# Four-layer convolution kernel on one core: the copies of the planes' edges behind layer 0's first loads, and the box's first part behind the transforms' products

## What is computed

```python
def reference(x, ...):
    x = x + _L0_conv_ref(_gn(x), ...)   # 1x1 and 3x3 convolution, product of 8x8 FFTs, normalization over channels
    x = x + _L1_conv_ref(_gn(x), ...)   # 1x1, FFT with a mask, 3x3, gelu gate
    x = x + _L2_conv_ref(_gn(x), ...)   # integral image, four gathered corners a pixel: the "box"
    x = x + _L3_conv_ref(_gn(x), ...)
    return x

def _gn(v, G=16, eps=1e-5):
    m = jnp.mean(g, axis=(2, 3, 4), keepdims=True)   # over the whole image
    s = jnp.var(g, axis=(2, 3, 4), keepdims=True)
    return ((g - m) / jnp.sqrt(s + eps)).reshape(v.shape)
```

## Time and profile before

| | before |
|---|---|
| median of three runs | 20823.17 us |
| lowest, highest | 20798.16, 20833.35 us |
| profiled execution | 20805.98 us |
| its span | 20804.4 us |
| PE, DVE, ACT, POOL busy | 91%, 64%, 36%, 50% |
| PE's granted clock, mean | 0.962 |

### The profile page before, as it was taken

How to read it: one execution, slowest core, us unless ns; L and a number is a source line. 1 busy time by engine, 2 the same in 40 slices (tenths; PEclk the granted TensorE clock), 3 DMA queues, 4 the chain that set the end, 5 groups by cost and what they waited for, 6 DMA issues and landing times. The chain is left out here.

```text
span 20804.4 us, 500656 instructions
## 1 busy us (share of the span) xinstructions
PE 18912.8 (91%) x172464; PEld 11734.2 (56%) x172464; DVE 13400.9 (64%) x22319; ACT 7497.1 (36%) x22720; POOL 10324.5 (50%) x8692
## 2 busy tenths in 40 slices
PE   6998998989999989899999898999997889898999
PEld 4665555466655554566555546665555456565666
DVE  4444445666667776666677766666777677777744
ACT  4664332155542221555422215553322122222222
POOL 0000000077767740777677407776773088787800
PEclk9999999999999999999999999999999999999999
DMA  3331112655544446555344465553444666666633
GB/s 94 72 72 44 36 37 92 135 114 116 114 102 113 114 126 137 116 120 119 100 113 112 129 134 118 119 120 101 113 116 128 136 145 147 151 150 148 151 87 77
DMA packets 932864, 2323.52 MB, mean 112 GB/s; under 512 B 276340, under 2 KB 528504, under 8 KB 844124
## 3 DMA queue, kind: packets, MB, share of 16 engines
q1 hardware_dynamic: 500560, 1364.68, 28.1%
q0 software_dynamic: 430080, 928.96, 16.9%
HBM read 1915.53 MB, written 385.13 MB: 111 GB/s over the span
## 5 line engine op out<-in xcount | busy, mean ns | idle before, releaser
L1842 POOL DMA_INDIRECT e_got<-table,e_idx x6144 | 7483.8, 1218 | 2376.3 <-issue 1624.3
L1858 POOL DMA_INDIRECT e_got<-table,e_idx x2048 | 2539.9, 1240 | 690.1 <-issue 537.0
L1012 PE MATMUL b_p_conv<-b_z,b_diag 32*32 32x512 f32 x76032 | 2810.7, 599 | 0.0
L531 PE MATMUL a_p_qk<-a_wst,a_stack 125*128 125x192 f32 x12288 | 2463.9, 337 | 273.0 <-ACT a_qh L662 212.3
L531 PEld LDWEIGHTS a_p_qk<-a_wst,a_stack 125*128 125x128 f32 x12288 | 2023.2, 191 | 709.0 <-issue 438.6
L1114 ACT ACTIVATE b_z<-b_p_z 128x256 f32<-128x256 f32 x2112 | 845.0, 400 | 3875.9 <-PE b_p_z L976 3522.7
L1896 DVE TENSOR_TENSOR e_got<-e_got,e_wt 128x1536 f32<-128x1536 f32 x1024 | 1779.0, 1753 | 698.5 <-DMA e_got<-table,e_idx 646.3
L976 PEld LDWEIGHTS b_p_z<-const,b_ym 128*128 128x128 f32 x8448 | 1149.8, 196 | 1199.0 <-issue 696.9
L1201 DVE TENSOR_TENSOR b_ym<-b_p_in,b_mask 128x512 f32<-128x512 f32 x1056 | 729.9, 691 | 1653.1 <-PE b_p_in L968 1652.9
L976 PE MATMUL b_p_z<-const,b_ym 128*128 128x128 f32 x8448 | 1524.7, 304 | 100.2 <-ACT b_z L1114 94.0
L2142 PE MATMUL d_p_v<-d_xs,d_ws 125*128 125x512 f32 x4608 | 1379.7, 447 | 59.7 <-issue 56.2
(11 more groups left out here) (291 smaller groups left out, 35717.4 us busy)
## 6 DMA issues: line engine op xcount, KB each, us to landing
e_got<-table,e_idx POOLq DMA_INDIRECT x8192
b_x<-planes SPq DMA_DIRECT2D x264, 395.1 KB
a_stack<-in_xp SPq DMA_DIRECT2D x256, 387.0 KB
c_stack<-planes SPq DMA_DIRECT2D x256, 387.0 KB
d_stack<-planes SPq DMA_DIRECT2D x512, 193.5 KB
table<-i_acc SPq DMA_DIRECT2D x256, 384.0 KB, 2.3
b_xr<-planes SPq DMA_DIRECT2D x264, 197.5 KB
planes<-b_out SPq DMA_DIRECT2D x264, 197.5 KB
```

What stands on the lines that cost most here:

```text
L531: m = pe.matmul(dst_, st[:, row, dx + 128 * t:dx + 128 * t + 128], wst[:, dx, 0:2 * C2], start=(dx == 0), stop=False)
L1012: mm = pe.matmul(p_conv[q // 2 * 2 + r % 2][BLK * c:BLK * (c + 1), :], diag[g][BLK * r:BLK * (r + 1), k, :], zs[BLK * r:BLK * (r + 1), g, ...
L1842: pool.indirect_dma_start(out=self.got[q][:, t, c * REC:(c + 1) * REC], out_offset=None, in_=self.flat, in_offset=bass.IndirectOffsetOnAxi ...
L1858: pool.indirect_dma_start(out=self.got[q][:, t, c * REC:(c + 1) * REC], out_offset=None, in_=self.flat, in_offset=bass.IndirectOffsetOnAxi ...
```

## The change

The six copies are taken out of the first block, with SP's wait for them. They become a function `set_edges`, which `layer0` of image 0 calls on SP right behind the first loads of `others`. The wait for the six stands at the end of SP's stream in that call. On DVE the box's part is called from two places: in steps with a back it stands where it stood, and in the first step, which has none, behind the two products.

```diff
-def layer0(env, src, dst, p, b, boxes=None, stats=None):
+def layer0(env, src, dst, p, b, boxes=None, stats=None, edges=None):
...
                         sp.dma_start(t[:], planes(src, i + 1, 0, CP, 1, SROWS)).then_inc(others_loaded[i], 16)
+                if edges:
+                    edges[0](sp)
...
                 for k in range(2):
                     sp.wait_ge(stored[k], ((b + 1) * U + 1) * 16)
+                if edges:
+                    sp.wait_ge(edges[1], 96)
...
+                def box_parts(u, k):
+                    for part in ((1, 2) if k % 2 else (0,)):
+                        boxes.part(dve, u, k // 4, k // 2 % 2, part)
+
                 def step(u, k, n, front, back, back2, turn_box):
...
-                    if boxes and front:
-                        for part in ((1, 2) if k % 2 else (0,)):
-                            boxes.part(dve, u, k // 4, k // 2 % 2, part)
+                    if boxes and front and back:
+                        box_parts(u, k)
...
                             dve.tensor_tensor(prod[k % 2][:, h, :, :].rearrange("p t c -> p (t c)"), bank[0:NPROD, 0:4 * C2],
                                               qh[:, h, :, :].rearrange("p t c -> p (t c)"), ALU.mult).then_inc(prod_ready, 1)
+                        if boxes and not back:
+                            box_parts(u, k)
...
                 sp.dma_start(const[:], cst).then_inc(const_loaded, 16)
-
-                for t in (p1, p2):
-                    sp.dma_start(t[:, :, 0, :], xp[:, :, 0, :]).then_inc(edges, 16)
-                    sp.dma_start(t[:, :, H + 1:H + 10, :], xp[:, :, H + 1:H + 10, :]).then_inc(edges, 16)
-                    sp.dma_start(t[:, 0, 1:H + 1, :], xp[:, 0, 1:H + 1, :]).then_inc(edges, 16)
                 sp.wait_ge(const_loaded, 16)
-                sp.wait_ge(edges, 96)
...
+        def set_edges(sp):
+
+            for t in (p1, p2):
+                sp.dma_start(t[:, :, 0, :], xp[:, :, 0, :]).then_inc(edges, 16)
+                sp.dma_start(t[:, :, H + 1:H + 10, :], xp[:, :, H + 1:H + 10, :]).then_inc(edges, 16)
+                sp.dma_start(t[:, 0, 1:H + 1, :], xp[:, 0, 1:H + 1, :]).then_inc(edges, 16)
...
-            layer0(env, xp, p1, args("a_"), 0, stats=stats)
+            layer0(env, xp, p1, args("a_"), 0, stats=stats, edges=(set_edges, edges))
```

## The result

The changed kernel takes **20777.66 us** (median of 14 runs, 20764.94 to 20791.91), the kernel before, run beside it, 20819.13 (14 runs). The ratio is 0.9979, with a 95% interval of 0.9971 to 0.9987: 41.5 us, or 0.21%, faster. A second series of the same two gave 0.9983 (0.9974 to 0.9992), 34.1 us. Forecast were 33.5 us less and a median of 20786, in a range of 20760 to 20814.

The account below looks back on a forecast made before the run. The start was taken to be bound by SP's wait for six copies, the first three steps of `layer0` with boxes by the gathers. 32.0 + 0 + 1.5 = 33.5 us less, median 20786, range 20760 to 20814.

Parts of the forecast that it names:

- The start: First block: without the wait for the six copies, the first load comes at 6.4 to 6.8 us, 32.0 us earlier.
- The copies' new place: Behind the first `others` loads in image 0's `layer0`: copies cost zero, margin 2.6 us, up to 10 us as upper end.
- Rival (a): In `layer0` of image 0, the copies make the next `others[0]` late beyond DVE's slack, costing up to 10 us; chance 13%.
- Rival (c): Copies share DMA engines with loads issued before them; the first step's `others[0]` lands at 219, 37.5 us lost; chance 4%.
- Part two: `weigh` behind the products in the first step of three `layer0` calls with boxes: 1.5 us gained in all.
- small term: First steps of `layer0` with boxes: 32nd gather 0.5 to 0.7 us earlier; 0.5 a call taken, 1.5 us in all.
- The 7.4 us of the second step: PE turns the second step's result at about 4228.0 instead of 4235.37; worth nothing, as the third step waits for gathers.
- Rival (b): In the three `layer0` calls with boxes the 7.4 us come through, gaining 3 x 6.5 us more; chance 8%.
- within 2: Sign: time from the first step's second `weigh` to the third step's, 25.35 us, should stay within 2 us of that.
- bound of 2 us a call: Bounds given for the reordered `weigh` in each `layer0` call with boxes: -2 and +2 us.
- The clock: PE starts third and fourth steps colder after idling; each could cost 1.5 to 3 us, covered by gather wait and slack.
- rival (d): In the three `layer0` calls with boxes the cold clock outweighs the gather's half microsecond, +2 us a call; chance 7%.

## Why the prediction was right, and where it was not

**The start: right.** The first load at 6.50 us lies in the forecast 6.4 to 6.8, with no wait for the copies. At the statistics' end only 26.1 of the 32 us were there, since the stage took 107.5 us from the first load on, against 101.5 before. The traces give no sign that the change causes that: with the two other runs of the old start it took 107.2 and 105.1, and with the other starts like the change's between 98.0 and 105.6. It scatters by itself, on waits of one or two microseconds for loads.

**The copies' new place: right, with a little more room than forecast.** They cost DVE's first step nothing (16.11 us against 15.24, 16.42 with the copies elsewhere). The last copy ended at 191.5 and the next `others[0]` landed at 193.9. With the 25.6 us added by which DVE's first read had moved, that is 217.1 and 219.5 in the old time, where 219 and about 222 were forecast. The margin was 4.9 us instead of 2.6. Rival (a) was a real mechanism: at the call's end it cost 9.71 us, and with twice the copies 27.57. There the load behind the copies waited for the four engines. By the Trainium skill (DMA: Bandwidth & Descriptors, "Why a DMA increments its semaphore by 16 and not by 1") a DMA takes the lowest-numbered engines, so that the four are among the seven. These traces agree: three of the load's seven engines were done some 19 us ahead of the other four, and with the copies late it was 39.9 us from the first copy to the load's landing against 39.3 worked out. Rival (c) fell for loads already issued: these earlier loads weren't held up. The same copies ahead of them cost 29.5 us.

**Part two: the mechanism right, the small term mis-sized.** The 7.4 us of the second step came through there: the turning begins 10.37 us behind the 16th gather (4207.13 - 4196.76), before 17.80, so 7.43 us earlier. The third step again waited for the 32nd gather, and nothing of the 7.4 was left by itself. Rival (b), 6.5 us a call, doesn't come: the third step's turning is 2.85 us earlier against the 16th gather (30.55 against 33.40). The step that failed is the one that said "I take 0.5 a call". I had spread 5.3 us of overrun evenly over 10 us of DVE work, and moved only the 1.3 us of `lower` out of the stretch. The overrun lies in single issues instead, and what counts is which operations follow each other. The first long issue went from 3.51 to 1.49 us and the one of the third step from 2.86 to 1.45, while one new overrun of 0.43 came. That makes 2.02 + 1.41 - 0.43 = 3.0, less 0.1 on the others: 2.9 us in the first call; by the intervals between the two `weigh` the three calls have 3.0, 2.5 and 2.9, together 8.4. Each is outside the "within 2" that I had given, and outside the bound of 2 us a call. Added to 32.0 it makes 40.4, near the 41.5 of the first series; the second, 34.1, doesn't confirm it, and no time here settles whether the 8.4 reach the end. Nor do the traces: counted from the 16th gather, the seventh step's turning is 2.5, 1.6 and 2.8 us earlier with the change, but 2.8, 0.8 and 0.4 with the box's part alone.

**The clock.** It behaved as feared, and most of its price was covered. Behind both waits PE was granted 0.50, which is 1.2 GHz. The two stretches of the changed kernel, from the turning in the second step and in the third:

```profile
4207.00:4211.00 4.00, 3.87 (x14) 3.78 (x15) 1.71 (x3) 1.59 (x4) 2.92 (x4) 0.50 0.26 74
4227.00:4231.00 4.00, 3.69 (x13) 3.60 (x14) 3.40 (x6) 1.77 (x4) 3.08 (x4) 0.50 0.26 74
```

Before, the same work behind the second step's turning was granted 1.00, in this stretch:

```profile
4235.00:4239.00 4.00, 3.63 (x24) 3.05 (x24) 3.56 (x5) 1.83 (x5) 3.39 (x3) 1.00 0.27 74
```

and 0.63 behind the third's. For the work from the second step's turning up to its next wait PE took 14.6 us (4207.13 to 4221.73), before 12.8; these 1.8 us lie ahead of the wait of 5.58 us and cost nothing. In the fourth step nothing covers them: from the third step's turning to the fourth's 14.25, 14.43 and 14.90 us went by in the three calls, before 13.58, 13.38 and 13.65. These 0.7 to 1.3 us are a part of rival (d)'s price, and less than what the gathers gave. Other runs of the same order took 13.3 to 14.8 us there, so it isn't paid every time.

**The numbers.** 20786 for 20777.66; 35% had been given to faster by over 0.2%, 63% to within 0.2%. The result, 0.21%, sits on that border. The 7 us by which part two was too small are about the distance between forecast and result. But that the forecast's median lies so near to both series, 8.3 us over the one and 3.3 under the other, is in part luck: medians of the same kernel are 12 us apart.

## What to carry to other kernels

A DMA that nothing needs soon goes behind the loads that are needed now, at a place where the queue is otherwise empty; ahead of one of them it cost here nearly all that its removal from the start had won. Reckon the copies' end against the next load behind them, since the margin is lost there first, in time on the shared DMA engines. Where an engine's wait is removed and a stream of transfers binds behind it, ask when that stream begins: the order of `weigh` was worth about 3 us a call, and the load that starts the gathers, moved to the head of its queue, about 20.

## What the runs showed of the hardware

**Held-up issues of gathers.** In the stretch of gathers 16 to 32 an indirect DMA's issue on POOL takes 0.95 us, but 1.27 to 3.51 where it begins beside DVE's operations with two inputs in SBUF, or just ahead of one, and each of the long ones ends 0.83 us behind the end of a DVE operation. Over the whole trace of the kernel before, 2668 of 8192 issues are longer than 1.04 us, the longest 6.91, and 2604 of these end 0.82 to 0.84 us behind such an end. For example, with the change 4200.52 + 1.49 = 4202.01, and the `weigh` ended at 4199.43 + 1.76 = 4201.19; with the weighing in the middle 4209.89 + 2.89 = 4212.78, and the `weigh` ended at 4210.21 + 1.75 = 4211.96. Mostly it is the operation that ran as the issue began (2284 of the 2668). The longest issues of the stretch passed it by: the last one began beside `a_t` (until 4210.29) and ended with the `weigh` behind it, and the old one of 3.51 us passed three ends and ended with the first `halve`. In both, an operation with one input in PSUM ran first and one with both inputs in SBUF came behind it before the issue's 0.95 us were over. Over the whole trace 92 issues began beside `a_t` with a `weigh` behind it in that time, and 82 of them were long. Why the one is passed and the other not was not tested.

The Trainium skill (GPSIMD Engine Reference, "Specifications") names the sharing with DVE's operations of two SBUF inputs. That section has no length for it: taken at the operations' full length it gave 1.3 us a call in the forecast, and 2.5 to 3.0 were measured.

**SP's issues slow down.** A plain DMA's issue takes 0.3 to 1 us on SP's timeline, but behind some forty others those of the copies took 2.48 to 6.83 us, and with twice the copies up to 12.43. At their late place the same six took 0.66 to 1.05 us. They lay in SP's idle time here; with twice the copies SP came to the next `others` 29 us later, but the four DMA engines were later still.

**The share of the DMA engines isn't their rate.** The loads of 49 planes ran at 130 to 139 GB/s with a share of 0.42 to 0.44, those split into 48 and one at 137 GB/s with 0.90.
